# Reordering GpSimd's five steps in the cross-attention phase of a fused transformer kernel

## The reference

```
x = x + LN(decoder_block(LN(x)))
x = x + LN(moe_block(LN(x)))

decoder_block(h):
    y  = LN(h)*g+b;  h = h + proj(causal_attention(y))          # 16 heads of 8 features
    y  = LN(h)*g+b;  h = h + proj(cross_attention(y, encoder))  # own mask and key bias
    y  = LN(h)*g+b;  h = h + gelu(y @ fc_w + fc_b) @ mlp_w + mlp_b   # 128 -> 512 -> 128
moe_block(z):
    shared SwiGLU expert + sum over the two best of 8 SwiGLU experts, weighted by softmax gates
```

## Time and profile before

| | value |
|---|---|
| median of three runs | 1644.99 us |
| the profiled execution's own time | 1647.01 us |
| its span | 1645.3 us |
| mean granted clock of TensorE | 0.954 |
| PE busy | 1434.1 us, 87% of the span |
| DVE busy | 1116.3 us, 68% |
| ACT busy | 987.8 us, 60% |
| POOL busy | 317.8 us, 19% |

### The profile page before, as it was taken

How to read it: one execution, slowest core, us unless ns; L and a number is a source line. 1 busy time by engine, 2 the same in 40 slices (tenths; PEclk the granted TensorE clock), 3 DMA queues, 4 the chain that set the end, 5 groups by cost and what they waited for, 6 DMA issues and landing times. The chain is left out here.

```text
span 1645.3 us, 39092 instructions
## 1 busy us (share of the span) xinstructions
PE 1434.1 (87%) x15448; PEld 877.4 (53%) x15448; DVE 1116.3 (68%) x3252; ACT 987.8 (60%) x1618; POOL 317.8 (19%) x428
## 2 busy tenths in 40 slices
PE   2667789989898989989898998989899898989887
PEld 1445564655555565655556465555646565555443
DVE  5557676767777776776777676677767667647344
ACT  2255675766757576675757576575757666571642
POOL 3421121211212121121212111121212112020120
PEclk7679999999999999999999999999999999998898
DMA  3334212122040402213040212204031211010000
GB/s 69 57 77 52 55 22 55 21 44 38 22 59 9 67 15 39 36 32 50 10 72 10 50 26 39 43 16 64 10 56 20 44 32 28 9 24 12 15 5 9
DMA packets 79214, 58.05 MB, mean 35 GB/s; under 512 B 11004, under 2 KB 78902, under 8 KB 79030
## 3 DMA queue, kind: packets, MB, share of 16 engines
q1 hardware_dynamic: 76726, 53.90, 18.8%
q10 hardware_dynamic: 2304, 1.64, 0.7%
HBM read 11.57 MB, written 4.19 MB: 10 GB/s over the span
## 5 line engine op out<-in xcount | busy, mean ns | idle before, releaser
L1025 DVE TENSOR_REDUCE chunkmax<-ps 128x3 f32<-128x384 f32 (+1 forms) x1024 | 508.6, 553 | 119.2 <-PE ps L1379 113.6
L711 ACT ACTIVATE probs<-ps 128x768 f32<-128x768 f32 (+1 forms) x512 | 406.0, 809 | 199.3 <-PE ps L1374 195.5
L1444 PE MATMUL ps<-zT,w 128*128 128x512 f32 x576 | 281.0, 602 | 6.5 <-ACT silu_a L728 4.8
L728 ACT ACTIVATE silu_a<-ps,b 128x512 f32<-128x512 f32 x144 | 98.7, 685 | 197.9 <-PE ps L1444 174.5
L1359 PE MATMUL ps<-k_op,q_op 48*128 48x256 bf16 x512 | 147.4, 290 | 64.4 <-DVE chunkmax L1025 50.8
L1166 DVE SCALAR_TENSOR_TENSOR h_open<-ps,b,silu_a 128x512 f32<-128x512 f32 x128 | 95.8, 749 | 123.6 <-PE ps L1444 111.3
L1444 PEld LDWEIGHTS ps<-zT,w 128*128 128x128 f32 x576 | 102.8, 191 | 114.6 <-issue 87.4
L1341 PE MATMUL ps<-q_op,k_op 51*128 51x256 bf16 x512 | 141.7, 277 | 25.2 <-POOL lower L499 9.3
L1480 PE MATMUL ps<-hT,w 128*128 128x512 f32 x288 | 149.3, 599 | 3.8 <-DVE hT L1172 3.0
L1359 PE MATMUL ps<-xk_op,xq_op 51*128 51x256 bf16 x512 | 143.5, 282 | 6.1 <-DVE chunkmax L1025 5.7
L1371 PE MATMUL ps<-mask_q_lo,ident_lo 64*128 64x256 bf16 x512 | 145.9, 288 | 0.0
(11 more groups left out here) (245 smaller groups left out, 3436.9 us busy)
## 6 DMA issues: line engine op xcount, KB each, us to landing
q_op<-q_parts SPq DMA_DIRECT2D x192, 64.0 KB
xq_op<-xq_parts SPq DMA_DIRECT2D x192, 64.0 KB
k_op<-k_parts SPq DMA_DIRECT2D x168, 64.0 KB
x_tm<-in_L_attn_hidden_states SPq DMA_DIRECT2D x16, 256.0 KB, 5.9
x_keep<-in_L_attn_hidden_states SPq DMA_DIRECT2D x16, 256.0 KB, 6.1
out<-o_tm SPq DMA_DIRECT2D x16, 256.0 KB, 2.3
k_op<-k_parts ACTq DMA_DIRECT2D x24, 64.0 KB
w<-in_L_ffn_rw SPq DMA_DIRECT2D x1, 1024.0 KB
```

What stands on the lines that cost most here:

```text
L711: act.activation(probs[:, four % 2, 2 * pair:2 * pair + 2, 0:T + a.seen], ps[:, 2 * (1 - g % 2):2 * (1 - g % 2) + 2, 0:T + a.seen], ACT.Ex ...
L1025: dve.tensor_reduce(chunkmax[:, b, at, :], ps[:, MAX_BANK[n], 0:3 * a.seen].rearrange("p (c n) -> p c n", c=3), AX.X, ALU.max).then_inc(a. ...
L1444: pe.matmul(ps[:, bank, :], w, src[:], start=True, stop=True).then_inc(sig.sem, 1)
```

## The change

The five jobs are the same; two of them move. `finish(i - 3)` goes from after `add_bias` to ahead of `rstd(ca, ...)`, and `add_bias(yb_tm, ...)` goes from before `finish` to the end, after `rstd(n_z, ...)`. No other engine's program is altered.

```diff
                 if exists(k) and k < LAST:
                     rstd(n_post, tiny_post, k)
-                if exists(i):
-                    rstd(ca, tiny2, i)
-                if exists(i + 1):
-
-                    add_bias(yb_tm, y_tm, bo, y_ready.done(i + 1), sa.h.before(i + 1), yb_ready)
                 if exists(i - 3):
                     finish(i - 3)
+                if exists(i):
+                    rstd(ca, tiny2, i)
                 if exists(k) and k < LAST:
                     sum_xn(k)
                     rstd(n_z, tiny_z, k)
+                if exists(i + 1):
+
+                    add_bias(yb_tm, y_tm, bo, y_ready.done(i + 1), sa.h.before(i + 1), yb_ready)
```

More of the change, by code:

```diff
@@ L612, in body @@
                     rstd(n_post, tiny_post, k)
+                if exists(i - 3):
+                    finish(i - 3)
                 if exists(i):
                     rstd(ca, tiny2, i)
-                if exists(i + 1):
-                    add_bias(yb_tm, y_tm, bo, y_ready.done(i + 1), sa.h.before(i + 1), yb_ready)
-                if exists(i - 3):
-                    finish(i - 3)
                 if exists(k) and k < LAST:
```

## The result

The changed kernel took 1628.74 us (median of four runs, 1625.95 to 1632.07) against 1645.62 us (four runs, 1643.63 to 1648.78) for the kernel before: a ratio of 0.9895, 95% interval 0.9874 to 0.9917. That is 16.9 us, or 1.05%, faster. The forecast was 1623 us with a range of 1618 to 1632 us. Timed again later beside fifteen runs of the kernel before, it took 1629.37 us against 1648.61, a ratio of 0.9878 (0.9863 to 0.9894), some 19 to 20 us.

The account below looks back on a forecast made before the run. PE (87% busy) was taken to wait in the cross phase on POOL's late `xn`, through DVE's statistics and next maximum. 1647.01 - 13.7 (wait) - 8.9 (clock) = 1624.4 us, stated as 1623 after allowing for the profile's offset; range 1618 to 1632 us.

Parts of the forecast that it names:

- The final sum first: POOL, cross phase: `o_tm` (1.27 us) fits into 2.98 us of idle time ahead of `rstd(ca)`; cost 0.
- The bias last: POOL, behind `tiny_z`: `yb_tm` (1.27 us) ends near 712.6 with 29 us of slack; cost 0.
- The sum `xn`: Cross phase, bodies 3 to 14: `xn` comes earlier, DVE's wait goes, PE's becomes 0.81 us; 12 x 1.14 = 13.7 us gained.
- The clock: Eight bodies' granted-clock falls behind PE's long wait vanish: 8 x 1.11 = 8.9 us gained, bounded below by 0.
- nowhere else: Through bodies 2 to 14, the granted clock falls only right behind PE's long wait in the cross phase.
- The sum: Whole kernel: profiled execution minus both gains, 1647.01 - 13.7 - 8.9 = 1624.4 us.
- The anchor: Starting time: profiled execution 2.0 us above the median; taken off in full 1622.4 us, left on 1624.4; said 1623.
- the rival at 1631.3 us: Cross phase: the wait goes but the eight clock falls stay; 1644.99 - 13.7 = 1631.3 us, chance 0.12.
- the one with 0.70: The forecast itself: `xn` wait and clock falls in the cross phase both go; 1623 us, chance 0.70.
- The full clock penalty: Slow-clock bodies: PE's 1.70 us per fall comes back in full; 1617.7 us, chance 0.06.
- hidden: Cross phase: DVE's saved time returns as a wait for PE or ACT; 1645 us, chance 0.04.
- The slower rival: POOL: `finish`, waiting for its inputs, holds up `rstd(ca)` and `xn` in 12 bodies; 30 us, 1675 us, chance 0.03.

Follow-up runs that it names:

- The doses: Changed kernel plus one add of 7, 8 or 12 blocks of 128 columns between `rstd(ca)` and `sum_xn`: 1633.72, 1640.36 and 1660.18 us.
- the run with the long hold: Changed kernel plus one GpSimd add of 12 x 128 columns between `finish` and `rstd(ca)`: 1658.94 us.

## Why the prediction was right, point by point

- *The final sum first, cost 0.* Right. 1.76 us of POOL's idle time are left where 1.7 were forecast. Its store costs nothing that shows. In body 15 it holds up DVE for 0.5 us; the prediction had no such term, but allowed for `rstd(ca)` coming a few tenths later there, at no cost.
- *The bias last, cost 0.* Right; it ends at 710.65, long before anyone needs it.
- *The sum `xn`.* Right on DVE (no wait in bodies 3 to 14) and on PE (0.81 us). It follows `rstd(ca)` by 0.19 us, put down to issue, and not within 0.1 us as I had said. PE's waits for `chunkmax` at line 1359 fell from 56.5 to 43.0 us over the profile, 13.5 of the 13.7 forecast.
- *The clock.* The value taken, all falls gone at this place, was right: none behind this wait in 48 bodies. The doses show that it was no luck of body 2. The reasoning had a gap: "nowhere else" was read from one profile, and three of the other profiles without long waits, besides the changed kernel's second, have a fall or two in the early cross phase, where PE's waits are 0.62 and 0.29 us.
- *The sum.* Forecast 13.7 + 8.9 = 22.6 us; the stretches gave 22.6, the middle as a whole 21.9 (first profiles) and 20.9 (second profiles). The missing 1 to 2 us are the falls elsewhere and small differences of the rest of the bodies.
- *The anchor.* It accounts for a part of the 5.7 us by which the forecast was too low. The median of three runs, 1644.99 us, was low: later medians of the same kernel were 1648.61, 1647.26, 1646.88 and 1647.45 us. I took the profiled execution's 2.0 us over the median for falls or accident of the profile, while the head alone moves it by 5 us between executions. From 1647.5, the forecast gain of 22.6 us gives 1624.9, so the low start explains about 2 of the 5.7 us. The smaller gain of the middle explains 1 to 2 more. The rest, some 2 to 3 us, is in the middle of neither pair of profiles; the head alone scatters by more than that, and no run settles it. The measured time lies in the range because the range took in the rival at 1631.3 us, not because the sum was close.
- *The rivals.* The falls did not stay (1631.3 us), though that number lies nearer to the measured 1628.7 than mine (2.6 us against 5.7). By time alone the rival with the chance of 0.12 would have won over the one with 0.70; the clock of the stretches decided it. The full clock penalty did not come back (1617.7 us): the stretches returned 1.1 us for each fall, as the rows had it, and not 1.7. Nothing was hidden. The slower rival was priced by delay on POOL alone; that `rstd(ca)` has room was right, but the run with the long hold shows that a step there has a second price that I did not know of. In the twelve full bodies the changed kernel escapes it, since `finish` ends at 700.67 and the first small `TENSOR_SCALAR` comes at 702.11; in body 15 it does not.

Left open: what decides whether the head takes 236 or 241 us, why falls appear now and then behind the short waits of the early cross phase (6 in 96 bodies), and what besides its length decides whether a wait is followed by a fall.

## What to carry to other kernels

Look for a body of the pipeline that lacks the step in question: body 2 gave the price of the change to a hundredth of a microsecond, before any run. It gave the price of that place, and not the kernel's time, which was 5.7 us off the forecast. An engine that is busy for 19% of the time can still set the pace where the others wait for what it makes. Once a first move has taken the late step out of the way, a second one buys margin only, so ask how much margin is left before adding it. Cut the profile into head, steady middle and tail before comparing two executions; a head that scatters by 5 us hides a quarter of such a gain.

## What was not expected of the hardware

- The granted clock fell to its half behind single PE waits, in 0 of 12 bodies at 1.34 us, 4 of 12 at 1.61, 16 of 24 at 1.95 and 10 of 12 at 2.69 us, all at one place. A fall cost the stretch about 1.1 us, and one of twice the length 2.4. At another place of the same phase it fell in 6 of 11 bodies behind 2.62 to 2.84 us.
- A DVE `TENSOR_SCALAR` of 128x4 took 2.19 us in place of 0.17 and ended with a GpSimd add of 128x1536 that shared no data with it. Beside eight short adds it took 0.26 us, and the one behind it 0.50.
